# Q stored twice by head parity out of PSUM, scores on 32-row tiles, all of V centred by TensorE

## What is computed

```python
q = layernorm(x); k = v = ctx
ig, fg = concat(q, k, v) @ Wi + bi, concat(q, k, v) @ Wf + bf      # per head
log_D = lower_triangle(cumsum(logsigmoid(fg)) differences) + ig
D  = exp(log_D - max(log_D))
C  = (q_h @ k_h.T) / sqrt(16) * D                                  # per head
h  = (C / max(|sum C|, exp(-max))) @ v_h
x  = x + tanh(g0) * headnorm(h) * ln_scale
x  = x + tanh(g1) * moe(layernorm(x))
```

## Time and profile before

| | us |
|---|---|
| median of three runs | 222.68 |
| lowest and highest of them | 222.11, 222.68 |
| span of the profiled execution, first to last instruction | 219.9 |

### The profile page before, as it was taken

How to read it: one execution, slowest core, us unless ns; L and a number is a source line. 1 busy time by engine, 2 the same in 40 slices (tenths; PEclk the granted TensorE clock), 3 DMA queues, 4 the chain that set the end, 5 groups by cost and what they waited for, 6 DMA issues and landing times.

```text
span 219.9 us, 4347 instructions
## 1 busy us (share of the span) xinstructions
PE 200.4 (91%) x1373; PEld 142.2 (65%) x1374; DVE 161.1 (73%) x354; ACT 140.4 (64%) x281; POOL 89.4 (41%) x96
## 2 busy tenths in 40 slices
PE   8999899989889898979999999999999999999930
PEld 3478554434346544468888888888888888888720
DVE  6897764688989889998777747767767777667520
ACT  2387878898964797746666645566566665665510
POOL 8100254338380000611555555555444555532232
PEclk9999999999999999999999999999999999999996
DMA  3999999921010124110222332334333233342212
GB/s 110 322 366 375 372 375 372 373 88 48 3 48 3 48 87 156 48 51 24 51 48 48 51 48 48 52 51 67 56 54 60 48 48 48 53 62 33 24 24 24
DMA packets 20034, 23.43 MB, mean 107 GB/s; under 512 B 3888, under 2 KB 15152, under 8 KB 20016
## 3 DMA queue, kind: packets, MB, share of 16 engines
q1 hardware_dynamic: 13696, 16.94, 22.4%
q0 software_dynamic: 4464, 6.16, 17.1%
q10 hardware_dynamic: 1856, 0.10, 0.6%
HBM read 17.95 MB, written 5.24 MB: 105 GB/s over the span
## 4 chain that ended last, share of the span: by engine, by line
PE 67%; DVE 16%; ACT 6%; DMA 4%; issue 3%; POOL 1%; DVEq 0%; ACTq 0%; POOLq 0%
PE bank L1446 28%; PE bank L1258 7%; PE bank L1466 6%; PE bank L1478 6%; PE bank L1457 5%; PE bank L1298 3%; PE bank L1469 3%; DMA x_sb<-in_x_dram 3%; ACT arena L511 2%; PE bank L1428 2%; DVE w_sb_r L973 2%; DMA out_dram<-hraw,sidx 2%; PE bank L1274 2%; PE bank L1179 1%; DVE st L801 1%
## 5 line engine op out<-in xcount | busy, mean ns | idle before, releaser
L1446 PE MATMUL bank<-arena_r,xn_sb_r 128*128 x176 | 54.6, 391 | 0.0
L471 POOL DMA_INDIRECT out_dram<-hraw,sidx x16 | 26.1, 1632 | 38.5 <-DVE hraw L1135 22.5
L1446 PEld LDWEIGHTS bank<-arena_r,xn_sb_r 128*128 128x128 f32 x176 | 33.1, 188 | 6.7
L1446 PE MATMUL bank<-w_sb_r,xn_sb_r 128*128 x88 | 36.5, 415 | 0.3 <-issue 0.2
L676 ACT ACTIVATE x_sb<-bank 128x512 f32<-128x512 f32 x23 | 13.8, 599 | 29.7 <-PE bank L1446 26.4
L432 POOL TENSOR_SCALAR_AFFINE_SELECT arena<-arena 128x1024 f32<-128x1024 f32 x16 | 17.6, 1102 | 36.5 <-ACT arena L541 36.5
L1086 DVE TENSOR_TENSOR x_sb<-x_sb,bank 128x512 f32<-128x512 f32 x23 | 15.8, 686 | 16.4 <-ACT x_sb L676 16.4
L1162 PE MATMUL bank<-ones_b 128*128 128x512 bf16 x103 | 25.6, 397 | 1.1 <-POOL ones_b L385 1.1
L454 POOL DMA_INDIRECT cvT<-xnorm_scratch,gidx x12 | 12.3, 1028 | 31.2 <-DVE gidx L1035 23.4
L851 DVE TENSOR_TENSOR arena<-bank,arena 128x1024 f32<-128x1024 f32 x16 | 19.5, 1222 | 6.8 <-POOL arena L432 6.6
L973 DVE TENSOR_TENSOR w_sb_r<-w_sb,arena_r 128x512 fp32r<-128x512 f32 x32 | 20.1, 683 | 0.1
(11 more groups left out here) (234 smaller groups left out, 403.9 us busy)
## 6 DMA issues: line engine op xcount, KB each, us to landing
w_sb<-in_L_ffn_w_dram SPq DMA_DIRECT2D x24, 512.0 KB, 9.4
x_sb<-in_x_dram SPq DMA_DIRECT2D x2, 512.0 KB, 6.7
arena<-in_ctx_dram SPq DMA_DIRECT2D x2, 512.0 KB, 9.3
out_dram<-x_sb SPq DMA_DIRECT2D x8, 128.0 KB, 1.8
xnorm_scratch<-xn_sb SPq DMA_DIRECT2D x8, 128.0 KB, 1.9
out_dram<-hraw,sidx POOLq DMA_INDIRECT x16, 3.8
cvT<-xnorm_scratch,gidx POOLq DMA_INDIRECT x12, 2.8
hraw<-xnorm_scratch,gidx POOLq DMA_INDIRECT x11, 2.8
```

The costliest lines, as they stand in the source:

```text
L471: nc.gpsimd.indirect_dma_start(out=out[:, :], out_offset=bass.IndirectOffsetOnAxis(ap=sidx[:, i:i + 1], axis=0), in_=y_sb[i % YBUF], in_of ...
L1446: last = nc.tensor.matmul(ps_scores[p][:, n, :], a, w, start=(k == 0 and j == 0), stop=(k == KC - 1 and j == 2))
```

## The change

- `qkT` is split: `kT` holds K, and `qp` two copies of Q per sequence and chunk, one with the rows of odd heads zeroed, one with those of even heads; both carry the factor 1/4. The copies are made out of PSUM: three pairs by ScalarE, one (n = 6) by VectorE. `mask_q` is gone. Gate weights for Q are multiplied by 4 to make up for the factor.
- A score's row tile has 32 rows, the two heads of which are told apart by the two copies. A step takes two row tiles `j` and both 128-channel chunks `c`: four matmuls against 256 columns, row tile `j` into bank `j`. The eight heads of a half are now four of each chunk (`half_heads`, and with it the tables of rows).
- The gates by Q multiply both copies (their sum is Q), so a half takes 8 matmuls by K and 16 by Q, in two functions.
- V of all four pairs is centred by TensorE; VectorE's part is gone.
- TensorE's order ahead of the loop is rewritten (at the end of the diff), `sum_router` moves ahead of the gates, and both first scores ahead of the first differences.
- `kT`, `qp` and `dec` lie at the upper end of `arena`, so the copies of the first expert's weights can be made earlier: they stand in ScalarE's loop at b = 3 to 6.

```diff
-    K_STORED = (1, 2, 5, 6)
-    Q_STORED = (3, 4, 7, 8)
-    GATES_AFTER = (4, 8)
+    RELEASED_BY = (1, 2, 4, 6)
...
-        widths = (B * 2 * KC * S, B * KC * 4 * S, 4 * HC * S)
+        widths = (B * KC * S, B * KC * 2 * S, 4 * HC * S)
+        below = E * W13 - sum(widths)
...
-        v_ps = (ps_h, ps_scores[1][:, 0, :])
+        v_ps = (ps_h, ps_scores[0][:, 0, :], ps_scores[0][:, 1, :], ps_h)
...
-        half_heads = [range(a * HC, (a + 1) * HC) for a in range(2)]
+        half_heads = [[c * HC + a * 4 + i for c in range(KC) for i in range(4)] for a in range(2)]
...
-            def mask_q(b, heads):
-                act.wait_ge(s_qks, Q_STORED[b // 2])
-                for h in heads:
-                    nc.scalar.activation(qm[:, b, :, h, :], qkT[:, b, 0:KC, :], ACT.Copy,
-                                         scale=pmask[:, h:h + 1]).then_inc(s_qm, 1)
+            def store_q(n, pair):
+                act.wait_ge(s_qkt, n + 1)
+                for odd in range(2):
+                    nc.scalar.activation(qp[:, 2 * pair:2 * pair + 2, :, odd, :],
+                                         pair_ps[n % 4].rearrange("p (b c s) -> p b c s", b=2, c=KC),
+                                         ACT.Copy, scale=pmask[:, odd:odd + 1]).then_inc(s_qks, 1)
...
-            store_pair(0, 1, 0)
-            store_pair(1, 1, 1)
-            store_pair(2, 0, 0)
-            store_pair(3, 0, 1)
-            store_pair(4, 1, 2)
-            store_pair(5, 1, 3)
-            store_pair(6, 0, 2)
-            store_pair(7, 0, 3)
+            store_k(0, 0)
+            store_k(1, 1)
+            act.wait_ge(s_pm, 1)
+            store_q(2, 0)
+            store_q(3, 1)
+            store_k(4, 2)
+            store_k(5, 3)
+            store_q(7, 3)
             softplus(0)
             softplus(1)
-            act.wait_ge(s_pm, 1)
-            mask_q(0, (0, 1, 2))
+            store_v(0)
+            store_v(1)
             store_a(0)
-            mask_q(0, (3,))
-            store_v(0)
-            mask_q(1, (0,))
+            store_v(2)
             store_a(1)
             decay(0)
-            store_v(1)
-            mask_q(1, (1, 2, 3))
+            store_v(3)
             decay(1)
...
             for b in range(B):
...
-                if b + 2 < B:
-                    mask_q(b + 2, (0, 1))
                 if 2 * b + 3 < 2 * B:
                     decay(2 * b + 3)
...
-                if b + 2 < B:
-                    mask_q(b + 2, (2, 3))
                 if 2 * b + 4 < 2 * B:
                     decay(2 * b + 4)
+                if b == 3:
+                    act.wait_ge(s_w[0], 16 * 3 * (E - LATE))
+                if 3 <= b < B - 1:
+                    upper_weights(0, b - 3)
...
-            act.wait_ge(s_sc, KC * B)
-            act.wait_ge(s_w[0], 16 * 3 * (E - LATE))
-            upper_weights(0, 0)
             guess_heads(NG - 1)
             store_xnT(2)
-            for k in range(1, SPLIT):
-                upper_weights(0, k)
...
+            nc.vector.tensor_scalar(wg_sb[:, 0:KC, :], wg_sb[:, 0:KC, :], float(DH) ** 0.5, None,
+                                    ALU.mult).then_inc(s_par2, 1)
-            vlate = ctx_sb[:, HB:, :].rearrange("p b (h d) -> p (b h) d", d=DH)
-            link(nc.vector.tensor_reduce(vsum[:], vlate, AX_X, ALU.add))
...
+            store_q(6, 2)
...
-                nc.vector.tensor_tensor(d, ps_scores[a].rearrange("p g n -> p (g n)"), d, ALU.mult).then_inc(s_cm, 1)
+                d = dec[:, n % 4].rearrange("p (c j i) s -> p c j (i s)", c=KC, j=2)
+                nc.vector.tensor_tensor(d, ps_scores[a].rearrange("p j (c n) -> p c j n", c=KC), d,
+                                        ALU.mult).then_inc(s_cm, 1)
...
+            def gates_by_q(i):
+                pe.wait_ge(s_qks, 10 if i else 6)
+                if i == 0:
+                    pe.wait_ge(s_par2, 2)
+                else:
+                    pe.wait_ge(s_qkd, 2)
+                for c in range(KC):
+                    for odd in range(2):
+                        for j in range(HB):
+                            last = nc.tensor.matmul(ps_scores[1][j * G2:(j + 1) * G2, i, 0:S], wg_sb[:, c, :],
+                                                    qp[:, HB * i + j, c, odd, :], start=False,
+                                                    stop=(c == KC - 1 and odd == 1), tile_position=(0, j * G2))
...
-                if a == 0:
-                    pe.wait_ge(s_qm, 4 * b + 4)
                 if n >= 2:
                     pe.wait_ge(s_cm, n - 1)
                 elif n == 1:
-                    pe.wait_ge(s_vp, 2)
-                    pe.wait_ge(s_wc, 1)
-                for g in range(2):
-                    r = slice(g * 64, (g + 1) * 64)
-                    last = nc.tensor.matmul(ps_scores[a][:, g, :], qkT[r, b, KC + a, :],
-                                            qm[r, b, a].rearrange("p k s -> p (k s)"),
-                                            start=True, stop=True, tile_position=(g * 64, 0))
+                    pe.wait_ge(s_gz, 2)
+                else:
+                    pe.wait_ge(s_vp, 3)
+                for c in range(KC):
+                    for j in range(2):
+                        r = slice((2 * a + j) * 32, (2 * a + j + 1) * 32)
+                        last = nc.tensor.matmul(ps_scores[a][:, j, c * 2 * S:(c + 1) * 2 * S], kT[r, b, c, :],
+                                                qp[r, b, c].rearrange("p u s -> p (u s)"),
+                                                start=True, stop=True, tile_position=((2 * a + j) * 32, 0))
...
             turn_pair(5, ctx_sb, 3)
+            sum_router()
             biases_of(0)
+            turn_pair(6, xn_sb, 2)
+            gates_by_k(0)
+            turn_pair(7, xn_sb, 3)
+            gates_by_q(0)
             biases_of(1)
-            turn_pair(6, xn_sb, 2)
-            turn_pair(7, xn_sb, 3)
-            gates_of(0)
-            gates_of(1)
+            gates_by_k(1)
+            gates_by_q(1)
+            center_v(0)
+            center_v(1)
             turn_rows(turn_i, gz, s_gz, 0)
             turn_rows(turn_f, fcum, s_fc, 0)
+            center_v(2)
             turn_rows(turn_i, gz, s_gz, 1)
             turn_rows(turn_f, fcum, s_fc, 1)
-            sum_router()
-            center_v(0)
-            center_v(1)
-            differences(0)
+            center_v(3)
             scores(0)
             scores(1)
+            differences(0)
             differences(1)
```

More of the change, by code:

```diff
@@ L98, in bass_gated_mlstm_moe_kernel @@
         arena, arena_r = placed("arena", [P, E * W13])
-        widths = (B * 2 * KC * S, B * KC * 4 * S, 4 * HC * S)
-        assert sum(widths) <= E * W13
-        qkT, qm, dec = (arena[:, sum(widths[:i]):sum(widths[:i + 1])] for i in range(3))
+        widths = (B * KC * S, B * KC * 2 * S, 4 * HC * S)
+        below = E * W13 - sum(widths)
+        assert EARLY * W13 <= below
+        kT, qp, dec = (arena[:, below + sum(widths[:i]):below + sum(widths[:i + 1])] for i in range(3))
         ctx_sb = dec[:, 2 * HC * S:]
@@ L203, in bass_gated_mlstm_moe_kernel @@
         hhflat = hh.rearrange("p b h d -> p (b h d)")
-        scratch = arena[:, sum(widths[:2]):sum(widths)]
+        scratch = arena[:, below + sum(widths[:2]):]
         sel, wsl, ecmp, slotk, beat = carve(scratch, [NS * 2 * NT // 2, NS * 3 * NT // 2, NT * E, NS * E, B * E * E])
@@ L1190, in biases_of, with gates_by_k @@
                                      tile_position=(0, j * G2))
-            def gates_of(i):
-                pe.wait_ge(s_qks, GATES_AFTER[i])
+            def gates_by_k(i):
+                pe.wait_ge(s_qks, 8 if i else 2)
                 if i == 0:
                     pe.wait_ge(s_par2, 1)
-                for c in range(2 * KC):
+                for c in range(KC):
                     for j in range(HB):
-                        last = nc.tensor.matmul(ps_scores[1][j * G2:(j + 1) * G2, i, 0:S], wg_sb[:, c, :],
-                                                qkT[:, HB * i + j, c, :], start=False, stop=(c == 2 * KC - 1),
-                                                tile_position=(0, j * G2))
+                        nc.tensor.matmul(ps_scores[1][j * G2:(j + 1) * G2, i, 0:S], wg_sb[:, KC + c, :],
+                                         kT[:, HB * i + j, c, :], start=False, stop=False,
+                                         tile_position=(0, j * G2))
@@ L1202, in gates_of @@
                 last.then_inc(s_gate, 1)
             def center_v(pair):
-                pe.wait_ge(s_qks, K_STORED[pair])
                 if pair == 0:
+                    pe.wait_ge(s_qks, 10)
+                    pe.wait_ge(s_qkd, 2)
                     pe.wait_ge(s_cen, 1)
-                else:
-                    pe.wait_ge(s_gz, 2)
+                if pair == 3:
+                    pe.wait_ge(s_vp, 1)
                 for j in range(2 * KC):
                     b, c = 2 * pair + j // KC, j % KC
```

(6 more changed lines are left out.)

58 lines of the change are left out of this document (29 added, 29 removed).

## The result

The changed kernel took **223.66 us** (median of 20 runs; 223.27 the lowest) against 222.10 of the kernel before (20 runs): a ratio of **1.0068, 95% interval 1.0057 to 1.0079**, or +1.5 us. The forecast was 225.7, +3.0. The direction held; about half of the size did not. Part of the 2.0 us between forecast and result is the starting point: three runs had given 222.68, twenty gave 222.10. (Every run listed since lies 1.7 to 1.9 us above its own span, so the 2.8 that the prediction added to the span of 219.9 was about 1.0 too much.) The rest, about 1.5 us, is in the trace.

The account below looks back on a forecast made before the run. TensorE, busy 91% of the span, was taken as close to full in the loop, its queue deciding ahead of it. 3.77 + 1.26 - 2.04 = +3.0; 219.9 + 3.0 + 2.8 = 225.7 us, range 222.9 to 227.6.

Parts of the forecast that it names:

- the order ahead of the loop: Ahead of the loop: TensorE's in-order queue, not the data, decides when the last turning starts, 23.5 instead of 19.9.
- The last turning: Ahead of the loop: the last turning of the gates' rows (L1223) starts 3.6 us later, its rows ready at 21.4.
- Two scores, 1.05 and 0.95: Ahead of the loop: the first two scores start at 25.7, then a change of shape; first differences load at 27.8.
- the first `cv`: At the loop's start: the first `cv` comes at 33.5 instead of 29.73, 3.8 us later.
- the loop's sum: In the loop: masked-copy waits removed save 2.0 us, shape changes at six odd scores cost 1.3 us.
- The unseen price: In the loop: switching from 64-row differences to 32-row scores costs 0 to 0.32 a step, taken as 0.21.
- the cover: In the loop: VectorE's product ends at 37.27, 1.9 before the scores at 39.20 that reuse its bank.
- Behind the loop the chain is VectorE's: Behind the loop: VectorE's chain is unchanged, so everything there moves along by one constant.
- (1): Rival, in the loop: ScalarE's queue sets the period, which falls to 4.6; -1.2 us, 221.5; chance 0.13.
- (2): Rival, in the loop: new shape changes cost nothing and half the cvT wait goes; 0.3 us, 223.0; chance 0.08.
- (3): Rival, in scores: 32-row groups do not run side by side, each lot streams twice as long; 237; chance 0.04.
- the first term of the sum, 3.77: Ahead of the loop: the delay of the first `cv`, 3.77 us, entering the sum 3.77 + 1.26 - 2.04.

Follow-up runs that it names:

- Experiment 1: The changed kernel with three of four centrings behind the turnings of the gate rows and the first differences ahead of the first scores; 222.34 us, 1.0013 to the kernel before.
- Experiment 2: The changed kernel with the second step's first scores put on the row groups of the first step's; 224.50 us, 1.0121 to the kernel before.
- experiment 3: The changed kernel with scores on 64-row tiles like differences, the first two steps sharing their tiles; 224.17 us, 1.0088 to the kernel before.
- experiment 4: The kernel before without its 24 masked copies of Q in the loop; 221.02 us, 0.9952 to the kernel before.
- experiment 6: The changed kernel with V of the last four sequences centred by VectorE again, two of four TensorE centrings undone; 223.69 us, 1.0051 to the kernel before.
- experiment 7: The changed kernel with V of the last four sequences on VectorE, plus nine filling matmuls around the first differences; 222.49 us, 1.0016 to the kernel before.
- experiment 5: The kernel before without masked copies in the loop and with VectorE's statistics moved from the loop to behind it; 223.29 us, 1.0025 to the kernel before.
- 8: The changed kernel with late V on VectorE, turnings right behind the first centring, and the second centring behind the first differences; 221.48 us, 0.9967 to the kernel before.
- 9: The changed kernel with late V on VectorE, turnings early, and the loop's scores issued in pairs on four row groups; 221.96 us, 0.9999 to the kernel before.

## Why the prediction was right and wrong

**Right: the order ahead of the loop.** The last turning was forecast at 23.53 and came at 23.25 net; it waited for no data, and the first scores waited for the third V eviction, as worked out. Experiment 1 changes nothing but the order there and takes 1.2 us back.

**Wrong, the step that failed: "Two scores, 1.05 and 0.95".** They were priced one behind the other, 2.0. The first step's row tiles are groups 0 and 1, the second's 2 and 3: the line `(2 * a + j) * 32` in the diff says so. Together they take 1.16, 0.84 less. The row from which the price came was a 64-row pair that fills the array. Experiment 2 puts the two one behind the other: 2.00, as priced, and everything behind comes 0.85 later. The Trainium skill, TensorEngine Tiling (Array Packing), Key Properties, says right behind the rule that the prediction weighed that tiles work independently, and that different ones can load and multiply in parallel. Here 1.16 against 2.00 bears it out, across two steps that the program issues one after the other.

**Smaller misses in the same chain.** The last turning came 0.28 earlier than forecast (23.25 net, not 23.53). From the router sum's first load to pair six's the prediction had 1.01 (14.07 to 15.08); 0.90 was measured (14.36 to 15.26), without idle time between router sum and biases, where it had put a change of shape. The rest of the 0.28 is spread over steps of under 0.1 each. From the first scores to the first differences it had 2.1 (25.7 to 27.8); one behind the other they take 1.93 (experiment 2), side by side 1.09. With all that the first `cv` is 1.2 earlier than forecast: 2.56 later than before, not 3.8.

**Right: the loop's sum.** From the first `cv` to the sixth sequence's transposes the forecast had -2.04 + 1.26 = -0.78; the traces show 29.95 against 30.76, -0.81. The unseen price, 0.21 for row tiles of 64 to 32, is 0.20 by experiment 3. That agrees with the Trainium skill's rule (TensorEngine Tiling (Array Packing), Key Properties) that changing the mode drains TensorE; for two sizes of row tile no row had shown anything when the prediction was made. But the two terms were each taken as worth their TensorE time, and they are not: alone the masks give 1.1 of 2.0 (experiment 4) and the missing switches 0.16 of 1.2 in the trace (experiment 3), because at a period of 5.06 VectorE's product comes late. At 5.27 the product that the odd scores at 60.15 need ends at 59.95 (58.73 + 1.22), just in time, so the change's net 0.8 got through. That was luck: the cover that the prediction read as 1.9 in an early sequence is 0.2 there. "Behind the loop the chain is VectorE's" was in the text; that this chain reaches into the loop was not.

**Rivals.** (1), a period of 4.6 set by ScalarE: it was 5.27. (2), free switches: 0.20 each, and TensorE's wait for cvT is 2.9 where it was 3.0. (3), row groups in turn: they run side by side, four of them.

**The sum.** +2.56 - 0.81 = +1.75 by the traces; the last product moved 1.56 net, the median 1.5. Of the 1.4 that were forecast too much, 1.2 lie in the first term of the sum, 3.77, which came to 2.56.

## What to carry to other kernels

Before pricing two instructions one behind the other, read which part of the array each uses: disjoint row groups overlapped here (1.16 against 2.00), even across steps. Moving cheap work to the engine that everybody waits for costs most where it lands ahead of a small link in the longest chain; reordering such a queue can bring as much as removing the work. And a saved wait is worth at most the slack of the next engine, which is read in the busiest sequence and not in the mean.

## What was not expected of the hardware

- The clock can fall in the middle of work. In experiment 6 TensorE was busy 1.80 of 4.00 us, and then ran at 1.2 GHz from 28 to 30. With nine filling matmuls it stayed at 2.4 GHz (experiment 7).
- A small VectorE instruction can take as long as a neighbour's large one. In experiment 5 a 128x32 operation took 1.16 us while POOL added, ending with it, and 0.19 when POOL was idle:

```profile
60.52 1.27 POOL L444 TENSOR_TENSOR x_sb<-x_sb,hh 128x512 f32<-128x512 f32 x1
...
60.68 1.16 DVE L882 SCALAR_TENSOR_TENSOR s<-s,floor 128x32 f32<-128x32 f32 x1
...
69.60 0.19 DVE L882 SCALAR_TENSOR_TENSOR s<-s,floor 128x32 f32<-128x32 f32 x1
```

The Trainium skill, SBUF — State Buffer, SBUF: two separate sides, says that VectorE, with two operands in SBUF, and a GpSimd instruction that reads SBUF share a pair of ports as a lock held for a whole instruction; these rows agree. In experiment 4 such an operation (L894, 1.00 in place of 0.19) stands right ahead of the product that TensorE waits for; that the wait would go without it is an estimate from these rows, and no run removes the collision alone.
- The router weights' landing sits at the head of TensorE's gates: by the profile it waited 0.59, 0.40 and 0.51 for them in the executions of experiments 6, 8 and 5 (the last is built on the kernel before), and not at all in those of 1, 7, 9 and the changed kernel.
